# A two-layer graph kernel: the first pair of row blocks cut into two blocks of half the rows

## The chip, the cores and the metric

The kernel runs on one core of one Trainium2 chip. The metric is device time of one execution in microseconds, lower is better. The engines are TensorE (PE in the profile, its weight loads PEld), VectorE (DVE), ScalarE (ACT), GpSimd (POOL, which also issues most transfers) and SyncE (SP).

## The reference, cut to what matters

`N = M = 4096` rows and columns, `D = 64` features. `adj` is a 4096 x 4096 matrix of 0 and 1 with about 0.2% ones.

```python
h = relu(layernorm(x))
s = (h @ W) @ a1                      # one score per row
t = (entity_embs @ W) @ a2            # one score per column
e = leaky_relu(s[:, None] + t[None, :], 0.2)
e = where(adj > 0, e, -9e15)
att = softmax(e, axis=1)              # 4096 x 4096
x = x + elu(att @ entity_embs + h)
h = relu(layernorm(x))
x = x + (adj == 1) @ h + h
```

## The kernel before

Everything is held transposed: columns of `adj` lie on the 128 partitions in 32 column tiles, rows lie along the free axis. The 4096 rows are four **pairs** of two **halves** of 512 rows (`HALF`), and a **block** is one pair (`HALVES = (2, 2, 2, 2)`). A **step** n is one column tile of one block, 128 columns by 1024 rows; there are 4 x 32 = 128 steps. `adj` arrives as bf16 in 64 **chunks** of 512 KB, 16 to a block, two steps to a chunk, in a ring of 24 slots (`am`). POOL issues them, chunk q into the slot of chunk q - 24 once the steps of that one are made.

Per step:

- DVE makes `yp` (L819): max of the row's score `s8b` and the column's `t8neg`, plus the mask in `am`. Its output has four buffers (`YS`), so step n waits until TensorE is through with step n - 4 (`pv_done`).
- ACT takes the exponential in place (L593).
- PE adds the tile to the block's numerator `acc2` (L1077) and, at every odd step, two tiles to the denominators `dens` (L1092).

The exponent needs a shift for each row, an upper bound on its scores over its neighbours. For a block of rows it comes from this chain, which needs all chunks of that block: PE sums `gtab` against `am` (`biggest`, L926), DVE reads the sums (`read_sums`, L693, L694), PE transposes (`turn`, L938), DVE takes maxima (`largest`, L700) and computes the shift (`shifts`, L707 to L722), PE spreads it over the partitions (`v_rows`, L946), ACT copies it to `vx` (L520), and DVE puts it into the masks with an exclusive or, two chunks at a time (`put_shift`, L735). `lone_rows` (L744) treats a special case. For blocks 1 to 3 the chain runs inside the steps of the block before, at step numbers from `sum_at`, `read_at`, `TURN`, `LARGEST`, `SHIFTS`, `VROWS`. For block 0 it runs ahead of step 0.

Ahead of step 0 stand two more chains. The column scores and their **extremes** lead over DVE and two small PE instructions (L1021, L1024) to `gtab` (L663 to L674). The first layernorm goes pair by pair: **centring** on PE (L1016), squares on ACT, `variance` on PE (L878), the power -1/2 and a diagonal matrix on POOL (`spread_out`, L423 to L425), `deviation` on PE (L885), `normed` on DVE (L640) to `h0`. From `h0` PE makes the row scores (`s_rows`, L906; `s_cols`, L913). PE also sums the entities (L1033, called esum here).

After a block's steps, `FIN` says at which steps of the next block its sums are inverted, weighted, added to `x`, normalized again and split into three bf16 parts `h3` (`inverses`, `spread`, `weighted`, `rows_on`, `centred`, `variance_again`, `normed_again`, `rests`, `lasts`).

The second layer is 32 **pieces** (`ORDER`), each one column group of 512 times one pair, four parts of six matmuls (`neighbours`, L1005). Eighteen are placed inside the steps by `PIECE_AT`, part i at step `PIECE_AT[v] + i`, and fourteen run after the last step. Pieces in `DIRECT` read the mask in the ring itself, so they must be done before `put_shift` changes that chunk: L733 makes DVE wait for them. Others get a copy of the mask by a transfer of its own (`edges`).

All order on an engine is the order of the code; each engine runs its list in order and waits on semaphores.

## Time and profile before

| what | value |
|---|---|
| median of 3 runs | 409.32 us (408.3 to 410.26) |
| the profiled execution | 408.06 us, span 406.3 us |
| PE busy | 350.4 us (86%) |
| DVE busy | 304.3 us (75%) |
| ACT busy | 183.1 us (45%) |
| POOL busy | 112.2 us (28%) |
| step 0 begins on DVE | 63.18 us |
| step 32 begins on DVE | 131.88 us |
| last step's matmuls end on PE | 362.7 us |

The span runs from the first to the last instruction of the core. Busy shares are means over the whole span, so the table says nothing about which engine ends last in a given stretch; for that the time-ordered views are read.

### The profile page before, as it was taken

The page shows a single profiled execution, that of the slowest core. Times are in us where ns is not written, and L with a number is a line of the kernel's source. Part 1 is how long each engine was busy: PE and PEld are TensorE (multiplying, and loading weights), DVE is VectorE, ACT ScalarE, POOL GpSimd, SP SyncE. Part 2 cuts the span into 40 slices and gives each one's busy share as a digit, 9 for nine tenths or more (in the row PEclk, how much of TensorE's full clock was granted, in tenths as well). Part 3 has the DMA queues.
Part 4 walks back from the last instruction along what each step waited for, and adds up shares of the span by engine and source line. Part 5 has one row for each costly group of instructions (what it writes and reads, how often), then busy time and mean ns, then how long its engine had stood idle before and what let it go on. Part 6 is the DMA issues. An engine that isn't in the chain of part 4 may idle for free.

```text
span 406.3 us, 5556 instructions
## 1 busy us (share of the span) xinstructions
PE 350.4 (86%) x2291; PEld 124.7 (31%) x2295; DVE 304.3 (75%) x303; ACT 183.1 (45%) x206; POOL 112.2 (28%) x165
## 2 busy tenths in 40 slices
PE   0568535999887779999898999997989999999996
PEld 0244211323121113233232332332323333334564
DVE  3282069968999998988999879699997899833211
ACT  1130114645646566744476556535556456532100
POOL 4189901101102114134311131202013199000500
PEclk9977955999999999999999999999999999999999
DMA  7999999875858987775598967999999990000011
GB/s 221 238 213 212 214 213 213 138 128 106 154 105 116 169 129 123 123 137 92 97 146 133 149 104 120 99 100 96 108 89 107 107 98 2 2 2 0 2 53 52
DMA packets 15848, 47.85 MB, mean 118 GB/s; under 512 B 1552, under 2 KB 1616, under 8 KB 15568
## 3 DMA queue, kind: packets, MB, share of 16 engines
q0 software_dynamic: 14656, 44.05, 71.1%
q1 hardware_dynamic: 1168, 3.46, 2.3%
q8 instruction: 18, 0.29, 0.3%
q14 instruction: 6, 0.05, 0.0%
HBM read 111.46 MB, written 1.05 MB: 277 GB/s over the span
## 4 chain that ended last, share of the span: by engine, by line
PE 51%; DVE 27%; issue 6%; POOL 6%; another core or an unknown queue 3%; ACT 3%; DMA 3%; SPq 1%; DVEq 0%; ACTq 0%
PE pb L1077 17%; DVE yp L819 15%; PE pb L1005 9%; PE pb L1092 8%; PE pa L1005 8%; DVE am L735 7%; DMA xs<-xt 3%; ACT yp L593 2%; POOL yp L425 2%; POOL rstd L424 2%; PE pa L926 2%; PE pa L906 2%; PE pb L1016 1%; PE pa L970 1%
## 5 line engine op out<-in xcount | busy, mean ns | idle before, releaser
L593 ACT ACTIVATE yp<-yp,tbias 128x1024 f32<-128x1024 f32 x128 | 146.3, 1149 | 112.6 <-DVE yp L819 110.6
L819 DVE SCALAR_TENSOR_TENSOR yp<-s8b,t8neg,am 128x1024 f32<-128x1024 f32 x128 | 160.9, 1295 | 15.3 <-PE pb L1092 14.7
L1077 PE MATMUL pb<-yp,enta 128*64 128x512 f32 x512 | 136.1, 617 | 24.3 <-ACT yp L593 23.4
L387 POOL DMA_DIRECT2D am<-adj_t x64 | 35.2, 557 | 151.7 <-DVE yp L819 151.3
L735 DVE TENSOR_TENSOR am<-am,vx 128x4096 uint16<-128x4096 uint16 x32 | 73.6, 2299 | 2.2 <-ACT vx L520 1.4
L1092 PE MATMUL pb<-yp,onesf 128*32 128x512 f32 x512 | 68.3, 605 | 0.1
L1077 PEld LDWEIGHTS pb<-yp,enta 128*64 128x64 f32 x512 | 29.1, 136 | 93.8 <-ACT yp L593 68.2
L1005 PE MATMUL pb<-am,h 128*64 128x512 bf16 (+1 forms) x432 | 55.1, 379 | 0.0
L1005 PEld LDWEIGHTS pb<-am,h 128*64 128x64 bf16 x432 | 26.3, 110 | 39.5 <-issue 28.7
L396 POOL DMA_DIRECT2D am<-adj_t x16 | 11.5, 717 | 61.6 <-DVE yp L819 61.6
L1005 PE MATMUL pa<-am,h 128*64 128x512 fp8e4 x240 | 28.2, 380 | 0.0
L926 PE MATMUL pa<-am,gtab 128*32 128x512 bf16 x256 | 19.7, 388 | 3.6 <-DMA am<-adj_t 3.6
L471 POOL TENSOR_TENSOR am<-am,eyeb 128x128 fp8e4<-128x128 fp8e4 x24 | 22.5, 971 | 0.0
L1092 PEld LDWEIGHTS pb<-yp,onesf 128*32 128x32 f32 x512 | 10.1, 108 | 36.9 <-issue 35.9
L1005 PEld LDWEIGHTS pa<-am,h 128*64 128x64 bf16 x240 | 14.5, 110 | 16.0 <-issue 7.7
L693 DVE TENSOR_SCALAR gmax<-pa,wk 128x1024 f32<-128x1024 int32 (+1 forms) x5 | 5.3, 1068 | 12.3 <-PE pa L926 12.3
L1016 PE MATMUL pb<-xs,mats 128*128 128x512 f32 x8 | 5.7, 880 | 9.6 <-DMA xs<-xt 9.6
L926 PEld LDWEIGHTS pa<-am,gtab 128*32 128x32 bf16 x256 | 6.5, 97 | 21.2 <-issue 20.7
L460 POOL TENSOR_SCALAR rstd<-rstd 128x8 f32<-128x8 f32 x4 | 1.0, 246 | 40.0 <-ACT rstd L548 40.0
L776 DVE TENSOR_TENSOR rs<-pa,rstd 128x512 f32<-128x512 f32 x4 | 2.8, 692 | 11.1 <-POOL rstd L461 11.1
L520 ACT CAST vx<-pa 128x512 bf16<-128x512 f32 x8 | 4.3, 580 | 13.6 <-remote 13.6
L640 DVE TENSOR_TENSOR h<-h,pb 128x512 f32<-128x512 f32 x4 | 2.7, 686 | 9.4 <-PE pb L885 9.4
(145 smaller groups left out, 259.4 us busy)
## 6 DMA issues: line engine op xcount, KB each, us to landing
am<-adj_t POOLq DMA_DIRECT2D x80, 512.0 KB, 7.7
edge<-adj_t POOLq DMA_DIRECT2D x4, 512.0 KB, 10.3
enta<-ent SPq DMA_DIRECT2D x1, 1040.0 KB, 5.2
xs<-xt SPq DMA_DIRECT2D x1, 1024.0 KB, 11.1
out<-yp SPq DMA_DIRECT2D x4, 256.0 KB, 2.0
mats<-eye SPq DMA_DIRECT2D x1, 256.0 KB, 6.7
wt_sb<-w_t SPq DMA_DIRECT2D x1, 32.0 KB, 2.2
a_sb<-a_cols SPq DMA_DIRECT2D x1, 0.5 KB, 2.1
```

The lines of the kernel that those rows point to most:

```text
L387: pool.dma_start(am[:, q % RING], adj_t[q]).then_inc(landed[q % RING], 16)
L396: pool.dma_start(edges(v).rearrange("p (c t) i -> p c (t i)", c=2), adj_t[q:q + 2].rearrange("c p n -> p c n")).then_inc(edges_in[v], 16)
L424: link(g.tensor_tensor(rstd0[:, p], rstd0[:, p], mhalf[:], ALU.pow))
L471: g.tensor_tensor(e, e, eyeb[:], ALU.add, saturate=False).then_inc(own_ready, 1)
L593: sc.activation(y, y, ACT.Exp, bias=tbias[:, at:at + 1]).then_inc(exp_done, 1)
L735: v.tensor_tensor(at, at, vx[:, b % 2, 0:width(b)].bitcast(U16).unsqueeze(1).to_broadcast([P, 2 * tiles(b), width(b)]), ALU.bitwise_xor).t ...
L819: v.scalar_tensor_tensor(out=yp[:, n % YS, 0:W], in0=s8b[:, b % 2, 0:W], scalar=t8neg[:, at:at + 1], in1=am[:, (chunk0[b] + c) % RING, jt ...
L926: mm = t.matmul(pa[g * KC:(g + 1) * KC, i], gtab[:, tile_at(b, jt)], am[:, (chunk0[b] + jt // T) % RING, at:at + HALF], start=(k == 0), st ...
L1005: mm = t.matmul(gather(v)[s * D:(s + 1) * D, :], h3[:, jt, k * D:(k + 1) * D], masks(v, i, s), start=(v in OPENS and i == 0 and k == 0), s ...
L1016: t.matmul(pb[:, p], centre, xs[:, p], start=True, stop=True).then_inc(x0_ps, 1)
L1077: t.matmul(acc2(b)[s * D:(s + 1) * D, :], enta[:, tile_at(b, jt), 0:D], yp[:, n % YS, s * HALF:(s + 1) * HALF], start=(jt == 0), stop=(jt ...
L1092: mm = t.matmul(dens[at:at + 32, :], onesf[:, 0:32], yp[:, (n - 1 + r) % YS, s * HALF:(s + 1) * HALF], start=(jt == 1), stop=(jt == NT - 1 ...
```

## The change

The first pair of rows becomes two blocks of one half each: `HALVES = (1, 1, 2, 2, 2)`. A chunk of such a block holds four column tiles of 512 rows, and a step takes two of them, so that a step is again 128 x 1024 elements and there are again 128 steps: block 0 is steps 0 to 15, block 1 steps 16 to 31, and blocks 2 to 4 are what blocks 1 to 3 were. Line numbers here are those of before.

- DVE and ACT issue two instructions of 512 instead of one of 1024 at each of steps 0 to 31.
- Block 0's shifts need 8 chunks. Block 1's chain is in block 0's steps: `read_sums` after step 4, `turn` at 5, `largest` and `shifts` after 7, `v_rows` at 8. For what is now block 2: sums at steps 6 to 24, then 25, 26, 28, 29.
- On PE the extremes' two instructions stand ahead of the centring, the centring of a pair between the variances, and `s_rows`, `s_cols` ahead of the esum.
- The two blocks' numerators and denominators are put together by four matmuls (`combined`) at step 34, copied out by ACT at 35. The end work of the first pair is two steps later each time, and the first six pieces start two steps later (`PIECE_AT` 49, 53, 59, 63, 69, 73 for 47, 51, 57, 61, 67, 71).
- `s_rows` of the next pair is one call for both halves, at steps 18, 48 and 78. POOL issues chunks 18 to 23 after its twelve small esum instructions.
- `mats` grows from four to five 128 x 128 matrices.

```diff
-HALVES = (2, 2, 2, 2)
+HALVES = (1, 1, 2, 2, 2)
...
+    NC_STEPS = [NT * m // 2 for m in HALVES]
+    start_of = [sum(NC_STEPS[:b]) for b in range(NB + 1)]
...
     def landed_at(q):
-        n = max(0, int((q - 16) * 1.2)) if q < 32 else 0
+        n = max(0, int(q * 1.29 - 15.5)) if q < 32 else 0
...
-        n = landed_at(chunk0[b] + (k + 1) * HALVES[b] - 1) + 1
+        n = landed_at(chunk0[b] + (k + 1) * HALVES[b] - 1) + (b >= 3)
...
-    SROWS = [(8, 10), (13, 15), (13, 15)]
-    TURN = [max(read_at(b + 1) - b * NT + 1, SROWS[b][-1] + 3) for b in range(NB - 1)]
+    SROWS = [None, 2, 16, 14]
+    TURN = [read_at(b + 1) - start_of[b] + 1 for b in range(NB - 1)]
     LARGEST = [t + 2 for t in TURN]
-    SHIFTS = [t + 3 for t in TURN]
+    SHIFTS = LARGEST
...
+        both = mats[:, 4, 0:D]
+        four = mats[:, 4, D:D + 32]
...
             def sums_out(b):
-                act.wait_ge(pv_done, (b + 1) * NT)
...
+                act.wait_ge(pv_done, start_of[b + 1])
+                if single(b):
+                    if b == 0:
+                        act.wait_ge(esp_ready, 1)
+                    sc.copy((tm, rs)[b][:], dens).then_inc(den_sb, 2)
+                    sc.copy((ta, num)[b][:], acc2(b)).then_inc(num_sb, 2)
+                    return
...
+            def combined():
+                act.wait_ge(comb_ps, 1)
+                sc.copy(inv, turned[D:P]).then_inc(inv_in, 1)
+                sc.copy(num[:], pb[:, 3]).then_inc(comb_sb, 1)
...
-                y = yp[:, n % YS, 0:width(b)]
-                at = tile_at(b, jt)
-                sc.activation(y, y, ACT.Exp, bias=tbias[:, at:at + 1]).then_inc(exp_done, 1)
+                m = 2 // HALVES[b]
+                for r in range(m):
+                    y = yp[:, n % YS, r * HALF:r * HALF + width(b)]
+                    at = tile_at(b, jt * m + r)
+                    e = sc.activation(y, y, ACT.Exp, bias=tbias[:, at:at + 1])
+                e.then_inc(exp_done, 1)
...
-            for p in range(NP):
-                normed(p)
+            normed(0)
+            normed(1)
             dve.wait_ge(eyeb_ready, 1)
             read_sums(0)
+            normed(2)
             largest(0, 0)
-            largest(0, 1)
             shifts(0)
             put_shift(0, 0)
             lone_rows(0)
+            normed(3)
...
+            def combined():
+                pe.wait_ge(num_sb, 4)
+                pe.wait_ge(den_sb, 4)
...
+                for s in range(2):
+                    t.matmul(pb[s * D:(s + 1) * D, 3], both, (ta, num)[s][:], start=True, stop=True,
+                             tile_position=(0, s * D))
+                for s in range(2):
+                    at = D + 32 * s
+                    mm = t.matmul(turned[at:at + 32], four, (tm, rs)[s][:], start=True, stop=True, tile_position=(0, at))
+                mm.then_inc(comb_ps, 1)
```

What the code's order now is on two engines, at the places that the prediction speaks of. The columns are line, operation, output <- inputs, size.

TensorE ahead of step 0, in the kernel before (`yp,onesf 64x512` is `deviation`, `am,gtab` is `biggest`, `enta` is the esum, `mats,m` and `d,onesf` are the extremes):

```order
L1016 MATMUL pb<-xs,mats 128x512 x4
L878 MATMUL pa<-mats,yp 128x2 x4
L1021 MATMUL pa<-mats,m 2x128
L1024 MATMUL pa<-d,onesf 128x2
L878 MATMUL pa<-mats,yp 128x2 x12
L885 MATMUL pb<-yp,onesf 64x512 x4
L1033 MATMUL pa<-enta,onesf 128x260 x8
L926 MATMUL pa<-am,gtab 32x512 x8
```

And of the change, from the same place to the point where the esum stands:

```order
L1097 MATMUL pa<-mats,m 2x128
L1100 MATMUL pa<-d,onesf 128x2
L1091 MATMUL pb<-xs,mats 128x512 x2
L936 MATMUL pa<-mats,yp 128x2 x4
L1091 MATMUL pb<-xs,mats 128x512
L936 MATMUL pa<-mats,yp 128x2 x4
L1091 MATMUL pb<-xs,mats 128x512
L936 MATMUL pa<-mats,yp 128x2 x8
L943 MATMUL pb<-yp,onesf 64x512 x2
L984 MATMUL pa<-am,gtab 32x512 x8
L962 MATMUL pa<-h,w 128x512 x2
L969 MATMUL pa<-w8s,h 128x2 x4
```

The extremes no longer stand behind the four centring matmuls, one pair's `deviation` instead of two is ahead of the first sums, and the row scores are ahead of the esum, which follows one call of `biggest` later.

VectorE from the first sums to the first step, in the kernel before (the seven small instructions of `shifts` stand between the two pieces shown):

```order
L693 TENSOR_SCALAR gmax<-pa,wk 128x512
L694 SCALAR_TENSOR_TENSOR gmax<-pa,gmax 128x512
L693 TENSOR_SCALAR gmax<-pa,wk 128x512
L694 SCALAR_TENSOR_TENSOR gmax<-pa,gmax 128x512
L700 TENSOR_REDUCE um<-pa 128x4 x2
...
L722 TENSOR_TENSOR vd<-eyeb,vb 128x512 x2
L735 TENSOR_TENSOR am<-am,vx 128x4096
L744 TENSOR_SCALAR rows<-vx 3x1024
L819 SCALAR_TENSOR_TENSOR yp<-s8b,t8neg,am 128x1024 x2
```

And of the change:

```order
L744 TENSOR_SCALAR gmax<-pa,wk 128x512
L745 SCALAR_TENSOR_TENSOR gmax<-pa,gmax 128x512
L694 TENSOR_TENSOR h<-h,pb 128x512
L751 TENSOR_REDUCE um<-pa 128x4
...
L773 TENSOR_TENSOR vd<-eyeb,vb 128x512
L786 TENSOR_TENSOR am<-am,vx 128x4096
L795 TENSOR_SCALAR rows<-vx 3x512
L694 TENSOR_TENSOR h<-h,pb 128x512
L876 SCALAR_TENSOR_TENSOR yp<-s8b,t8neg,am 128x512 x4
```

One half's chain is left ahead of step 0, and `normed` of pairs 2 and 3 (`h<-h,pb`) stands between its parts.

TensorE where the first pieces of the second layer begin, in the kernel before, from step 47 (`am,h 64x512` is a part of a piece, `yp,enta` the numerator of a step):

```order
L1077 MATMUL pb<-yp,enta 64x512 x2
L1005 MATMUL pb<-am,h 64x512 x6
L1092 MATMUL pb<-yp,onesf 32x512 x4
L1077 MATMUL pb<-yp,enta 64x512 x2
L1005 MATMUL pb<-am,h 64x512 x6
```

And of the change, from step 46 (the first row holds steps 46 and 47):

```order
L1161 MATMUL pb<-yp,enta 64x512 x4
L1176 MATMUL pb<-yp,onesf 32x512 x4
L962 MATMUL pa<-h,w 128x512 x2
L1161 MATMUL pb<-yp,enta 64x512 x4
L1082 MATMUL pb<-am,h 64x512 x6
```

The first part of piece 0 moved from step 47 to step 49, so its last part is now in step 52 and that of piece 1 in step 56. The masks that these two read are changed by DVE's `put_shift` behind steps 53 and 57 in both kernels.

## Rows read from the trace of the kernel before

**Rows 1.** The page: span, and one engine line and one group.

```profile
span 406.3 us, 5556 instructions
...
PE 350.4 (86%) x2291; PEld 124.7 (31%) x2295; DVE 304.3 (75%) x303; ACT 183.1 (45%) x206; POOL 112.2 (28%) x165
...
L926 PE MATMUL pa<-am,gtab 128*32 128x512 bf16 x256 | 19.7, 388 | 3.6 <-DMA am<-adj_t 3.6
```

**Rows 2.** Windows (steps 0-31, 32-63): PE, PEld, DVE, ACT, POOL busy; clock, DMA, GB/s.

```profile
63.18:131.88 68.70, 60.42 (x367) 16.47 (x370) 62.89 (x56) 38.46 (x37) 9.32 (x17) 0.95 0.78 134
131.88:204.90 73.02, 64.97 (x407) 18.81 (x406) 67.68 (x64) 42.10 (x46) 20.19 (x26) 1.00 0.74 123
```

**Rows 3.** The chain that ended last: start us, us, what.

```profile
14.31 5.71 PE pb L1016 x8
...
39.35 1.91 POOL yp L425
41.30 1.08 PE pb L885 x4
42.93 1.06 PE pa L906 x4
44.53 1.00 PE pb L913 x8
45.73 13.60 another core or an unknown queue
```

**Rows 4.** Timeline up to the first step (start us, us, engine, line).

```profile
12.19 0.15 DVE L650 TENSOR_SCALAR m<-m 128x1 f32<-128x1 f32 x1
...
23.28 1.79 DVE L664 TENSOR_SCALAR kq<-kq 128x32 f32<-128x32 f32 x1
...
27.55 1.22 DVE L674 TENSOR_TENSOR gtab<-gtab,pw 128x1024 bf16<-128x1024 bf16 x1
...
32.98 5.00 PE L1033 MATMUL pa<-enta,onesf 128*128 128x260 f32 x16
...
50.53 1.04 PE L926 MATMUL pa<-am,gtab 128*32 128x512 bf16 x8 [3.60 <-DMA am<-adj_t]
...
56.49 0.17 DVE L707 TENSOR_SCALAR vq<-um 128x8 f32<-128x8 f32 x1
...
59.34 1.19 ACT L520 CAST vx<-pa 128x512 bf16<-128x512 f32 x2 [13.62 <-remote]
60.64 2.29 DVE L735 TENSOR_TENSOR am<-am,vx 128x4096 uint16<-128x4096 uint16 x1 [1.39 <-ACT vx L520]
...
63.18 2.46 DVE L819 SCALAR_TENSOR_TENSOR yp<-s8b,t8neg,am 128x1024 f32<-128x1024 f32 x2
```

**Rows 5.** Three windows of 3 us, columns as in group 2.

```profile
24.00:27.00 3.00, 2.25 (x15) 2.16 (x14) 2.79 (x8) 1.27 (x4) 2.84 (x5) 0.71 1.08 216
...
33.00:36.00 3.00, 3.00 (x10) 2.46 (x9) 0.69 (x1) 0.00 (x0) 2.92 (x2) 0.58 1.08 214
...
69.00:72.00 3.00, 3.00 (x24) 0.90 (x24) 2.56 (x4) 2.30 (x3) 0.53 (x1) 0.90 0.99 178
```

**Rows 6.** DVE groups by shape: one over the whole run, one of steps 0-31.

```profile
L694 DVE SCALAR_TENSOR_TENSOR gmax<-pa,gmax 128x512 f32<-128x512 int32 x2 | 1.4, 692 | 0.1
...
L819 DVE SCALAR_TENSOR_TENSOR yp<-s8b,t8neg,am 128x1024 f32<-128x1024 f32 x33 | 40.8, 1279 | 5.6 <-PE pb L1092 5.3
```

**Rows 7.** Timeline of DVE, then of PE, around steps 53 and 57.

```profile
179.62 2.29 DVE L735 TENSOR_TENSOR am<-am,vx 128x4096 uint16<-128x4096 uint16 x1
...
186.31 1.28 DVE L693 TENSOR_SCALAR gmax<-pa,wk 128x1024 f32<-128x1024 int32 x1 [1.70 <-PE pa L926]
...
191.16 2.29 DVE L735 TENSOR_TENSOR am<-am,vx 128x4096 uint16<-128x4096 uint16 x1
...
178.36 0.82 PE L1005 MATMUL pb<-am,h 128*64 128x512 bf16 x6
...
182.52 0.82 PE L1005 MATMUL pb<-am,h 128*64 128x512 bf16 x6
```

420 lines of the change are left out of this document (230 added, 190 removed).

## The prediction

> **What bounds the kernel now.** I read the page first. TensorE is busy for 350.4 of 406.3 us [rows 1], so time can only come out of its first quarter or out of its work. The windows by steps come next: in steps 0 to 31 VectorE is busy 62.89 of 68.70 us and TensorE 60.42; in steps 32 to 63 it is 67.68 and 64.97 of 73.02 [rows 2]. Both are nearly full, VectorE a little more. Since step n needs step n - 4's buffer back, neither runs away from the other, and an earlier step 0 moves everything behind it, the tail too, as long as no new wait stands in the way. Third, the chain that ended last shows what sets step 0: centring until 20.0, POOL's diagonals until 41.26, then `deviation`, the row scores and the column scores on TensorE (1.08, 1.06, 1.00 us), and then 13.6 us that the view gives to an unknown queue [rows 3]. The timeline says what that is: TensorE waits 3.60 us for the last chunk of the block, which ends at 50.53, and its last sums end at 51.57; from there sums, transposes, maxima, shifts, the copy to `vx` and the first `put_shift` lead to step 0 at 63.18 [rows 4]. So the last chunk of 16 ends the wait, and behind it come 11.6 us that nothing covers.
>
> **Part 1: when step 0 starts.** Only 8 chunks are needed. The transfers run at 216 GB/s [rows 5], 2.4 us for 512 KB; chunk 15 landed at 50.5, so chunk 7 lands near 31. That is ahead of what follows, so the transfers no longer decide, and three chains must be followed.
>
> *Extremes.* Their values are ready at 12.34 [rows 4], but their matmuls stood behind the centring that ended at 20.0 [rows 3] and the first variance, and `gtab` was done at 28.77 [rows 4]. Turned at once, they gain 8.2 us: 20.5, or 19 if L664's 1.79 us (its neighbours of the same size take 0.2; it ran beside POOL's diagonal) goes too. Not last any more.
>
> *Centring.* Variance 0 now waits for two of four centrings, between half of 5.71 and, at the lower clock of their start, 3.4 us; it comes 2.3 to 2.9 us earlier and so do POOL's four diagonals: the fourth is ready near 39. The fifth matrix of `mats` is 64 KB, 0.3 us. TensorE has the four variances behind it near 25.3, `deviation` 0 at 26.4, and VectorE's multiplication (0.69, as L694 of that size [rows 6]) gives `h0` at 27.1.
>
> *TensorE's list from there.* `s_rows` 1.06 and `s_cols` 1.00 [rows 3]; 3 calls of four sums, at 19.7/256 us a matmul [rows 1] 0.3 each, the first two while `h0` is made: 29.5. Then the esum. It took 5.00 us from 32.98 [rows 4], half of it at the lower clock: the mean granted was 0.71 in 24 to 27 and 0.58 in 33 to 36 [rows 5], which puts the rise at 35.5. That is 2.5 us at 1.2 GHz and 2.5 at 2.4, so 3.75 if all at 2.4 and 7.5 if all at 1.2. I take 3.75, because in the new order TensorE has no hole longer than 1 us between 14.3 and here, where before its clock fell after holes: 33.2. `deviation` 1 is 1.1, five calls of sums 1.5: 35.8.
>
> *Behind the last sums.* Before: 51.57 to 63.18, 11.6 us. Up to the shifts at 56.49 it was 4.9 us for two halves in turn; for one it is two reads of 0.7, four transposes of 1.1 together and a maximum of 0.7 = 3.6, so 1.3 less. ACT's 1.19 us for two copies [rows 4] becomes 0.6. Added: `normed` 3 with 0.7, and 0.4 for small VectorE instructions beside POOL's last diagonal. `deviation` 2 and `normed` 2 lie beside the reads and the transposes: cost 0.7 without that cover. 11.6 - 1.3 - 0.6 + 0.7 + 0.4 = 10.8, so step 0 at 46.6: **16.6 us earlier**. Bounds: 45 (quick turns at 2.4 GHz) to 52 (esum at 1.2 GHz and 2 us for the rest of TensorE's list).
>
> **Part 2: steps 0 to 31.** Block 1's own chain, once ahead of step 0, is now in VectorE's steps: reads 1.4, maximum 0.7, small ones and one `vd` 2.1, lone rows 0.3: **+4.5 us** on the fuller engine. TensorE gets half a block's sums (2.5), transposes and shift row (1.0) too; it had 8.3 us free [rows 2] and loses the slack, no more. Two instructions of 512 for one of 1024: L694 takes 0.692 at 512 and L819 1.279 at 1024 [rows 6]. By durations that is 0.10 for each of 32 steps, 3.4 us; by starts (63.18 to 65.58 for two steps, 1.20 each [rows 4], against 0.61 for a 512) 0.6. These run unlinked, so I take the starts more: **+1.0**. ACT has 30 us free [rows 2]; 32 more instructions cost nothing. VectorE's waits, 5.8 us (68.70 - 62.89), 5.6 of them in front of L819 [rows 6], were made where TensorE had sums, row and column scores in steps 5 to 12 together; these are spread now, but block 0's sums and transposes come while TensorE is still at 1.2 GHz, and `read_sums` stands right behind step 4: 4.5 left, **-1.3**, bounds -4 and +3.
>
> The Trainium skill, page "VectorE: DVE Perf Modes", section on the TRN2 errata, speaks against this split: an instruction that reads SBUF pays a fixed cost each time, by its table 58 cycles at 0.96 GHz on VectorE. By it the split would be 1.9 us instead of my 1.0, an estimate from that page; the rows lie on both sides of it.
>
> **Part 3: steps 32 to 47.** `combined` is two matmuls like a step's numerator and two like its denominators, 2.0 us on TensorE; one VectorE instruction of 0.7 goes. It stands at step 34, where TensorE in steps 32 to 63 has 8 us free [rows 2], and behind it in the queue waits step 34's numerator, whose buffer VectorE needs at step 38. ACT's two copies replace three. **+0.3**, 2.0 without the cover. The end work's two steps of delay reach only `h3`, and the pieces move with it.
>
> **Part 4: a new wait at steps 53 and 57.** Before, piece 0 ended at 179.2 and `put_shift` behind step 53, which needs it, began at 179.62: 0.4 us of margin though three steps lie between, because TensorE trails. Now piece 0 ends in step 52. The part of a piece in that step ended at 183.3 [rows 7]; with two parts fewer ahead of it (0.75 each) it would be at 181.8. VectorE gets there at 178.2 to 179.6 and waits 2.2 to 3.6 us. What is behind it in its queue is step 54, for which TensorE runs dry; the 1.70 us that VectorE later waited for the sums [rows 7] is saved, so some 0.5 us is lost. At step 57 nothing is saved: piece 1 ends in step 56, and VectorE, which began that `put_shift` at 191.16 without a wait, waits about 2.1. Together **+2.6**, bounds 0 (TensorE trails less) and 5. Later pieces keep their margins.
>
> **Sum.** -16.6 + 4.5 + 1.0 - 1.3 + 0.3 + 2.6 = -9.5. The profiled execution took 408.06, so 398.6; it lies 0.3% below the median of 409.32, and for the median of the new kernel I give 399.
>
> **Rivals.**
>
> *The clock falls as before (0.2).* In 24 to 27 the mean was 0.71 [rows 5]. If it falls at 25 again, the esum costs 3.75 more and what stands around it up to 2: step 0 near 52, 404. For: each variance still waits for ACT. Against: the list between is full.
>
> The Trainium skill, page "TensorE: Matmul & The Clock Gate", section "What's actually happening", says that the low clock is the default and activity releases it. By that rule the fuller list holds 2.4 GHz and the forecast stands; the fall at 25 after a sparse stretch agrees.
>
> *The waits shrink more (0.2).* Without part 4's wait and with 2.5 us less in part 2: 394. For: pieces start later, so TensorE trails less.
>
> *The transfers decide after all (0.08).* By 2.4 us each, chunk 12 lands at 43 and is needed near 45, chunk 17 at 55.5 for step 6 near 60, chunk 23 at 70 for step 14 near 77. One that comes 3 us after its need gives 402. Against: POOL issues 18 to 23 while 16 and 17 are still on their way.
>
> *Slower: TensorE stays at 1.2 GHz in the first two blocks (0.05).* Step 0 comes when TensorE has been nearly idle for 8 us, and the small blocks hold VectorE longer per step. At 1.2 GHz two steps cost it some 6.6 us (3.7 and 2.0, and a share of sums) against 4.4 for VectorE: 1.1 a step. After 9 steps the gain is gone, with all 32 it is 433. Against: 1.00 was not far after step 0, the mean of 69 to 72 was 0.90 [rows 5], six to nine us behind the start of step 0.
>
> The forecast has 0.47. Its own range is 395 to 402; the range that leaves out 2 in 10 takes in the fall of the clock and most of the shrinking: 392.5 to 404.5. Measurement tells 0.5%, 2 us, from no change. Faster 0.94, within 0.03, slower 0.03: the last two are the long stay at 1.2 GHz and a stack of the bounds.
>
> **What would show it.** Right: first L876 near 46.6, esum of 3.6 to 4 us, no TensorE wait for a chunk of more than 1 us, step 32 near 119.5 and a wait of 2 to 4 us on PE in front of `put_shift` behind steps 53 and 57. Wrong: a first step after 50, a step 32 more than 73 us behind step 0, or TensorE idle behind step 100 for more than before.

## The result and the profile after

The changed kernel takes 407.83 us (median of 20, 404.77 to 414.96) against 408.29 (median of 20, 407.26 to 410.3) for the kernel before. The ratio is 0.9948, with a 95% interval of 0.9925 to 0.9971: 2.1 us faster, where 399 us had been forecast. Six of the 20 executions, 412.5 to 415.0 us, are left out of the ratio as slow ones; over all twenty the medians differ by 0.5 us and the means not at all (408.6 us both).

The profiled execution took 405.43 us, the one of before 408.06. The page of the changed kernel, its head and some lines of the 40 slices:

```profile
span 403.6 us, 5645 instructions
PE 353.0 (87%) x2303; PEld 122.1 (30%) x2303; DVE 307.0 (76%) x342; ACT 190.3 (47%) x241; POOL 119.1 (29%) x165
PE   1697597889879897987898999997989999999996
DVE  3804899899989998787699888898998999823211
PEclk9989799999989989998699999999999999999999
```

Against [rows 1] TensorE is busy for 2.6 us more, VectorE for 2.7, ScalarE for 7.2 and GpSimd for 6.9. What is new is in the line PEclk: behind the first quarter, where before nothing but 9s stood, there are falls in the slices near 120, 140 and 190 us, and in the last of them PE shows 7 and 8 and DVE 7 and 6.

The windows by steps, up to step 0, steps 0 to 31, 32 to 63, and 64 to 95. Columns: window, its length, then busy us and instructions of PE, PEld, DVE, ACT and POOL, the mean granted clock, the DMA share and GB/s.

```profile
0.00:45.88 45.88, 28.42 (x148) 14.22 (x148) 20.92 (x47) 8.71 (x21) 31.81 (x54) 0.93 0.98 222
45.88:121.58 75.70, 63.27 (x383) 16.39 (x385) 71.28 (x100) 45.49 (x72) 22.05 (x29) 0.95 0.94 176
121.58:204.65 83.07, 72.07 (x430) 19.82 (x428) 69.30 (x65) 44.40 (x48) 18.09 (x27) 0.92 0.66 109
204.65:281.90 77.25, 72.47 (x494) 23.82 (x494) 68.76 (x66) 43.93 (x48) 13.95 (x20) 1.00 0.91 115
```

Step 0 starts at 45.88 instead of 63.18: 17.3 us are won. Steps 0 to 31 then take 75.7 us instead of 68.7, and steps 32 to 63 take 83.1 instead of 75.4 (the window in [rows 2] ends at 204.90, where the `put_shift` ahead of step 64 starts; step 64 itself began at 207.26). That is 7.0 and 7.7 us given back. By the starts of step 48, 168.6 before and 158.5 now, nearly all of the second loss lies in steps 48 to 63: steps 32 to 47 take 36.9 us for 36.8, and steps 48 to 63 take 46.2 for 38.6. From step 64 to the end both kernels take the same time within 0.1 us. So the sum is -17.3 + 7.0 + 7.7 = -2.6, the difference of the profiled executions.

The timeline to step 0 (start, duration, engine, line, operation; count; idle time before it and what ended it):

```profile
14.77 3.68 PE L1091 MATMUL pb<-xs,mats 128*128 128x512 f32 x4 [0.70 <-DMA xs<-xt]
18.06 1.23 DVE L728 TENSOR_TENSOR gtab<-gtab,pw 128x1024 bf16<-128x1024 bf16 x1
19.09 1.10 PE L1091 MATMUL pb<-xs,mats 128*128 128x512 f32 x2
30.11 3.77 PE L1121 MATMUL pa<-enta,onesf 128*128 128x260 f32 x16
34.81 1.26 PE L984 MATMUL pa<-am,gtab 128*32 128x512 bf16 x20
42.75 2.32 DVE L786 TENSOR_TENSOR am<-am,vx 128x4096 uint16<-128x4096 uint16 x1 [1.17 <-ACT vx L559]
45.88 2.72 DVE L876 SCALAR_TENSOR_TENSOR yp<-s8b,t8neg,am 128x512 f32<-128x512 f32 x4
45.99 7.62 POOL L478 TENSOR_TENSOR esum<-esp,mats 128x65 f32<-128x65 bf16 x1
```

The table is ready at 19.3 instead of 28.8, the sum over the entities takes 3.77 us instead of 5.00, and no sum waits for a chunk: the wait of 3.60 us in [rows 4] has no successor. TensorE's clock did fall here too, from 25.0 to 28.5 us, but it was up again before the esum. The same view at steps 53 to 63, VectorE's waits and TensorE's holes:

```profile
172.78 2.29 DVE L786 TENSOR_TENSOR am<-am,vx 128x4096 uint16<-128x4096 uint16 x1 [3.73 <-PE pb L1082]
184.52 2.29 DVE L786 TENSOR_TENSOR am<-am,vx 128x4096 uint16<-128x4096 uint16 x1 [2.21 <-PE pb L1082]
189.24 1.98 PE L1161 MATMUL pb<-yp,enta 128*64 128x512 f32 x4 [2.55 <-ACT yp L644]
194.43 1.98 PE L1161 MATMUL pb<-yp,enta 128*64 128x512 f32 x4 [1.76 <-ACT yp L644]
199.55 2.48 DVE L876 SCALAR_TENSOR_TENSOR yp<-s8b,t8neg,am 128x1024 f32<-128x1024 f32 x2 [3.81 <-PE pb L1176]
```

VectorE waits 3.73 and 2.21 us for pieces 0 and 1, as predicted. But there is a third line of that kind: at 199.55 it waits 3.81 us for a buffer, for TensorE. Windows of 5 us show what stands ahead of it:

```profile
180.00:185.00 5.00, 5.00 (x38) 2.00 (x34) 2.79 (x3) 2.30 (x2) 0.57 (x1) 1.00 0.64 108
185.00:190.00 5.00, 2.45 (x20) 0.69 (x20) 4.90 (x8) 1.62 (x2) 0.00 (x0) 0.89 0.42 83
190.00:195.00 5.00, 3.00 (x8) 0.50 (x6) 4.86 (x9) 1.72 (x2) 1.49 (x3) 0.50 0.03 3
195.00:200.00 5.00, 5.00 (x22) 1.07 (x20) 1.19 (x2) 2.58 (x4) 2.27 (x4) 0.59 0.91 161
```

While VectorE stood at `put_shift`, it issued no step; TensorE ran dry behind it (2.45 of 5 us busy from 185 on), and then its granted clock went to 0.50, the level of 1.2 GHz. Four of its step matmuls took 1.98 us instead of 1.08 and it was late in its turn, and VectorE waited once more. By this trace one wait brings another; how far that holds is what the experiments ask.

### The profile page after: what moved, and what is told of

Read it like the earlier page. It is cut to its first block, busy times and chain, and to the rows that moved or that the text cites. A ratio compares the mean times of both kernels' runs of the same rounds, so it can differ in the third digit from the quotient of the medians.

```text
span 403.6 us, 5645 instructions
## 1 busy us (share of the span) xinstructions
PE 353.0 (87%) x2303; PEld 122.1 (30%) x2303; DVE 307.0 (76%) x342; ACT 190.3 (47%) x241; POOL 119.1 (29%) x165
## 4 chain that ended last, share of the span: by engine, by line
PE 54%; DVE 27%; issue 7%; ACT 6%; DMA 3%; POOL 1%; SPq 1%; DVEq 0%; ACTq 0%
PE pb L1161 17%; DVE yp L876 14%; PE pb L1082 9%; PE pb L1176 9%; PE pa L1082 8%; DVE am L786 6%; ACT yp L644 4%; DMA xs<-xt 3%; PE pa L984 2%; PE pb L1091 1%; DVE um L751 1%; PE pa L1047 1%; PE pa L1053 1%; PE pa L962 1%; PE pa L1121 1%
## 5 line engine op out<-in xcount | busy, mean ns | idle before, releaser
L644 ACT ACTIVATE yp<-yp,tbias 128x1024 f32<-128x1024 f32 (+1 forms) x160 | 152.1, 975 | 123.0 <-DVE yp L876 121.5
L876 DVE SCALAR_TENSOR_TENSOR yp<-s8b,t8neg,am 128x1024 f32<-128x1024 f32 (+1 forms) x160 | 164.7, 1075 | 15.8 <-PE pb L1176 15.3
L1161 PE MATMUL pb<-yp,enta 128*64 128x512 f32 x512 | 138.8, 627 | 28.8 <-ACT yp L644 28.4
L1176 PE MATMUL pb<-yp,onesf 128*32 128x512 f32 x512 | 70.7, 625 | 0.0
L1161 PEld LDWEIGHTS pb<-yp,enta 128*64 128x64 f32 x512 | 29.2, 137 | 97.4 <-ACT yp L644 68.7
L1176 PEld LDWEIGHTS pb<-yp,onesf 128*32 128x32 f32 x512 | 10.2, 109 | 38.5 <-issue 36.9
L984 PE MATMUL pa<-am,gtab 128*32 128x512 bf16 x256 | 21.5, 416 | 0.0
L499 POOL TENSOR_SCALAR rstd<-rstd 128x8 f32<-128x8 f32 x4 | 1.5, 387 | 38.1 <-ACT rstd L599 38.1
L500 POOL TENSOR_TENSOR rstd<-rstd,mhalf 128x8 f32<-128x8 f32 x4 | 10.4, 2604 | 0.3
L919 DVE SCALAR_TENSOR_TENSOR yp<-pa,xs 128x512 f32<-128x512 f32 x2 | 1.4, 692 | 10.0 <-PE pa L1082 10.0
L478 POOL TENSOR_TENSOR esum<-esp,mats 128x65 f32<-128x65 bf16 x2 | 8.3, 4127 | 0.2
```

What stands on the lines that cost most here:

```text
L478: return g.tensor_tensor(dst, esp[:, 0], eyef[:, k:k + 1].to_broadcast([P, D + 1]), ALU.mult)
L500: g.tensor_tensor(rstd[:], rstd[:], mhalf[:], ALU.pow).then_inc(rstd_ready, 1)
L644: e = sc.activation(y, y, ACT.Exp, bias=tbias[:, at:at + 1])
L876: y = v.scalar_tensor_tensor(out=yp[:, n % YS, r * HALF:r * HALF + W], in0=s8b[:, pair(b) % 2, cols(b)], scalar=t8neg[:, at:at + 1], in1=a ...
L984: mm = t.matmul(pa[g * KC:(g + 1) * KC, first[b] % 2 + i], gtab[:, tile_at(b, jt)], am[:, (chunk0[b] + jt // T) % RING, at:at + HALF], sta ...
L1161: t.matmul(acc2(b)[s * D:(s + 1) * D, :], enta[:, at, 0:D], yp[:, n % YS, s * HALF:(s + 1) * HALF], start=(jt == 0), stop=final, tile_posi ...
```

## The experiments

Theory A: what is missing lies in part 4, the pieces that end one step before their `put_shift`, with the fall of TensorE's clock that follows. Rivals: the price of the split (C), block 1's own chain (D), the pair's combination. In the diffs, a kernel is called by what it starts from.

**b_pieces_late: part 4 alone, in the kernel before.** It has the six changed places of the pieces and nothing else.

```diff
-PIECE_AT = (47, 51, 57, 61, 67, 71, 79, ...
+PIECE_AT = (49, 53, 59, 63, 69, 73, 79, ...
```

> The kernel before with nothing changed but the first six pieces two steps later (49, 53, 59, 63, 69, 73). Theory A, the late pieces: VectorE's put_shift behind steps 53 and 57 now waits for pieces that end in steps 52 and 56, TensorE then runs dry and its clock falls; this alone costs what the changed kernel gave back in steps 32 to 63, so 411 to 415 us against 408.3, with two waits of 2 to 4 us on PE in front of L735. Theory B, the rest of the change (the earlier start, the joining of the two blocks, the fuller VectorE) makes TensorE idle and the clock fall: then this kernel stays at 408 to 409.5, with waits in front of L735 but no fall of the clock.

414.25 us against 408.07, ratio 1.0166 (1.014 to 1.0193). The two rows of its timeline:

```profile
181.74 2.29 DVE L735 TENSOR_TENSOR am<-am,vx 128x4096 uint16<-128x4096 uint16 x1 [3.74 <-PE pb L1005]
193.48 2.29 DVE L735 TENSOR_TENSOR am<-am,vx 128x4096 uint16<-128x4096 uint16 x1 [2.22 <-PE pb L1005]
```

They are the waits of the changed kernel to 0.01 us, and there were none in [rows 7]. The move of the pieces costs 6 us by itself, in a kernel that has none of the rest. That is A's total, but its profile (5.1 us longer) shows only a part of A's way. Steps 48 to 63 grow by 3.8 us here, against 7.5 in the changed kernel. The clock falls once behind the second wait, for 3.4 us from 198.3, where the changed kernel has it low for 10.2 us from 188.9, and VectorE's third wait, of 3.81 us, is missing. Another 1.7 us arise in steps 64 to 95, which the changed kernel doesn't lose; no run shows why. So A holds for the two waits; that they alone bring the third is not shown.

**a_pieces_48 and a_put_later: the wait taken away in the changed kernel, in two ways.** The first lets pieces 0 and 1 start one step earlier. The second leaves them and puts off block 2's two xors that need them.

```diff
-PIECE_AT = (49, 53, 59, ...
+PIECE_AT = (48, 52, 59, ...
```

```diff
-                if jt % SUB == 1 and c + 2 < HALVES[b] * NQ:
+                later = {21: None, 25: None, 22: 12, 27: 14} if b == 2 else {}
+                if jt in later:
+                    if later[jt] is not None:
+                        put_shift(b, later[jt])
+                elif jt % SUB == 1 and c + 2 < HALVES[b] * NQ:
```

> The changed kernel with pieces 0 and 1 at steps 48 and 52 in place of 49 and 53, so that each ends two steps ahead of the put_shift that needs it and not one. Theory A: most of the two waits (3.7 and 2.2 us) goes and the clock does not fall near 189 us: 399 to 402 us against 405.3. Theory B: the waits go, but the clock falls all the same and VectorE waits elsewhere: 404 to 405.5.

> The changed kernel with the two put_shift calls that wait for pieces moved on VectorE, from behind steps 53 and 57 to behind steps 54 and 59; the pieces stay where they are. Theory A: the waits shrink to under 1 us and the time is 399 to 403 us, though put_shift, reads and shifts now stand closer together, which can starve TensorE once for 2 us. Theory B: 404 to 406.

405.77 us, ratio 0.9896 (0.9856 to 0.9936), and 405.3 us, ratio 0.9884 (0.9843 to 0.9926). The waits at `put_shift` are down to 1.09 and 0.35 us, but only 2.1 and 2.5 us of the 6 came back; A had expected 399 to 403. Both intervals still overlap that of the changed kernel, the second one barely. In a_pieces_48 B's signs came. TensorE waited 1.73 us at 190.85 for the `vd` of the next block's shifts, the clock fell at 192.5 all the same, and VectorE waited at step 62:

```profile
197.40 2.48 DVE L876 SCALAR_TENSOR_TENSOR yp<-s8b,t8neg,am 128x1024 f32<-128x1024 f32 x2 [2.87 <-PE pb L1176]
```

In a_put_later the clock holds there and that wait is gone. Steps 32 to 63 take 78.4 us, and two waits for TensorE stand behind a stretch at 1.2 GHz from 158.0 to 164.8:

```profile
168.36 2.48 DVE L876 SCALAR_TENSOR_TENSOR yp<-s8b,t8neg,am 128x1024 f32<-128x1024 f32 x2 [3.17 <-PE pb L1180]
172.95 1.28 DVE L876 SCALAR_TENSOR_TENSOR yp<-s8b,t8neg,am 128x1024 f32<-128x1024 f32 x1 [2.11 <-PE pb L1180]
```

**b_split: the two instructions of 512 alone, in the kernel before**, for steps 0 to 31 on VectorE and ScalarE.

```diff
-                v.scalar_tensor_tensor(out=yp[:, n % YS, 0:W], in0=s8b[:, b % 2, 0:W], ...
+                w = HALF if b == 0 else W
+                for r in range(W // w):
+                    e = jt % T * W + r * w
+                    y = v.scalar_tensor_tensor(out=yp[:, n % YS, r * w:(r + 1) * w], ...
```

> The kernel before with each instruction of 1024 on VectorE and ACT in steps 0 to 31 issued as two of 512, nothing else. In the changed kernel two such instructions start every 1.33 us against 1.20 for one. Theory C: this price is the split's own, 0.13 us a step on the fuller engine, so steps 0 to 31 take 4 us longer and the time is 411.5 to 413. Rival D: the steps got longer by block 1's chain and its waits; the split itself costs 1 us or less and the time is 408.5 to 409.5.

412.93 us, ratio 1.0114 (1.0093 to 1.0136). Its windows for steps 0 to 31 and 32 to 63:

```profile
63.03:134.23 71.20, 60.61 (x369) 16.09 (x370) 66.85 (x88) 44.35 (x69) 9.28 (x17) 0.96 0.77 132
134.23:209.52 75.29, 67.30 (x429) 19.50 (x428) 69.87 (x65) 43.66 (x47) 21.39 (x28) 1.00 0.74 124
```

Against [rows 2] VectorE is busy for 3.96 us more, 0.124 us for each of 32 steps, and its waits shrink by 1.5, so the stretch grows by 2.5 us. This is near the bound that the durations gave (0.10), not the one that I took from the starts. C is right for a part. The whole kernel lost 4.6 us by the ratio and 3.4 in the profiled execution. Steps 32 to 127 take what they took before; 1.2 us of the 3.4 lie behind the start of the last step (51.7 us for 50.6), and no run shows why.

**a_combined_twice: the pair's combination made twice.**

```diff
-                for s in range(2):
+                for s in (0, 1, 0, 1):
```

> The changed kernel with the four matmuls that put the pair's parts together made twice (the second pass writes the same values over the first): some 2 us more of TensorE work at step 34. The prediction costed one pass at +0.3 us, 2.0 without cover. If cover holds, the time stays within 1 us of 407.8 and step 48 within 0.5 us of 158.5. If the 2 us come through, step 48 is near 160.5 and the time near 410; then one pass is worth about 2 us and a part of what steps 32 to 63 took too long.

407.89 us, ratio 1.0002 (0.9968 to 1.0035); step 48 at 159.4 and step 64 at 205.7 us, where the two profiles of the changed kernel have 158.5 and 158.0, 204.6 and 206.1. Counted from step 32, step 48 comes 1.1 and 1.7 us later than in those two, so a part of the 2 us came through there; at the end it isn't told from none (this kernel's interval and the changed one's just overlap). What lets this rival fall is the changed kernel itself: steps 32 to 47, with the combination in them, take 36.9 us for 36.8 before.

**b_extremes_first and a_order_back: the order of the front, alone in the kernel before, and taken back in the changed one.**

```diff
+            pe.wait_ge(m2_ready, 1)
+            t.transpose(turned[0:2, 2 * P:3 * P], m2[:, 0:2], eyef).then_inc(m2t_ps, 1)
...
             pe.wait_ge(ld_x, 16)
             for p in range(NP):
                 t.matmul(pb[:, p], centre, xs[:, p], start=True, stop=True).then_inc(x0_ps, 1)
             variance(0)
-            pe.wait_ge(m2_ready, 1)
-            t.transpose(turned[0:2, 2 * P:3 * P], m2[:, 0:2], eyef).then_inc(m2t_ps, 1)
```

> The kernel before with one part of the change alone: TensorE turns the extremes ahead of the centring. The blocks stay. By the prediction the last chunk of the first block (landed at 50.5 us) sets step 0, so the table of ready values should come some 8 us earlier (near 20 us instead of 28.8) and step 0 stay within 0.5 us of 63.2: time within 0.5% of the kernel before. Rival: the earlier sums shift POOL's and TensorE's work so that step 0 moves by 2 us or more, and the halved first block is not what the 17.3 us come from alone.

> The changed kernel with TensorE's order of before in the front: four centrings and a variance, then the extremes, then the other variances. The table of ready values comes near 28 us instead of 19.3; the row scores and the sums of block 0 wait for it. By the prediction's chains the list behind the table (row and column scores, sums, colsum, 8 us) then starts at 28 instead of 26: step 0 at 47.5 to 50, 2 to 4 us later, and the time 2 to 4 us over the changed kernel's beside it. Rival: the esum and the diagonals of POOL hide it, step 0 within 0.7 us of 45.9, and the order of the extremes is worth nothing here either.

In the kernel before the new order gives nothing: 410.25 us, ratio 1.0024 (1.0003 to 1.0046). Its timeline has the table at 19.2, and then the same wait for the same chunk:

```profile
17.99 1.22 DVE L674 TENSOR_TENSOR gtab<-gtab,pw 128x1024 bf16<-128x1024 bf16 x1
50.74 1.04 PE L926 MATMUL pa<-am,gtab 128*32 128x512 bf16 x8 [3.98 <-DMA am<-adj_t]
63.39 1.27 DVE L819 SCALAR_TENSOR_TENSOR yp<-s8b,t8neg,am 128x1024 f32<-128x1024 f32 x1
```

In the changed kernel, taking the order back costs more than the 2 to 4 us expected: 413.28 us beside 409.51 for the changed kernel in the same set, 5.0 us by the two ratios (1.009, 1.0053 to 1.0127, against 0.9968), and in the profiled execution, the longest of the eight, step 0 8.3 us later:

```profile
19.51 0.95 PE L936 MATMUL pa<-mats,yp 128*128 128x2 f32 x8
27.19 1.23 DVE L728 TENSOR_TENSOR gtab<-gtab,pw 128x1024 bf16<-128x1024 bf16 x1
35.70 6.59 PE L1119 MATMUL pa<-enta,onesf 128*128 128x260 f32 x16
54.19 2.72 DVE L876 SCALAR_TENSOR_TENSOR yp<-s8b,t8neg,am 128x512 f32<-128x512 f32 x4
```

Block 0's first sums start at 28.84 instead of 26.08. The table, ready at 28.4, explains 2.3 us of that at most: the sums begin right behind `deviation`, without a wait. The other 5.5 us arise behind them, where TensorE had gone to 1.2 GHz at 24.4 us and stayed there until 41.4 (the sum over the entities takes 6.59 instead of 3.77 us). So the order is worth something only with the halved block; the halving brings step 0 from 63.18 to 54.19 without it. By this one execution the larger part of what the order brings goes with the clock; no run has the one without the other. b_extremes_first showed the price of a fall too, by chance. Its 12 executions are 407.85 to 408.42 at a mean granted clock of 0.962 (five) and 410.22 to 410.71 at 0.954 (seven). The profiled one is of the second kind, and its clock falls at 153 us, where that of [rows 2] had held 1.00. Its steps 32 to 47 take 38.1 us for 36.8, with a new wait of VectorE for a buffer of 1.30 us at 157.98. So this stretch, 3.4 us at 1.2 GHz, costs some 1.4 us. The 2.1 us between the two groups hold more than this one stretch: a mean clock 0.008 lower is some 6.5 us at 1.2 GHz, and the lower group has no profile.

**a_fill and a_later_fill: TensorE kept busy in its holes.** Matmuls with all-zero weights are added to a sum that is open, so nothing but TensorE's time changes. The first is the changed kernel (4 to 6 such matmuls ahead of steps 29, 46, 54, 58, 59), the second a_put_later (ahead of 29, 46, 59, 60).

```diff
+                if n in FILL:
+                    pe.wait_ge(zeros_in, 1)
+                    for _ in range(FILL[n]):
+                        t.matmul(acc2(b)[0:D, :], zeros[:], gtab[:, 0:HALF // KC].rearrange("p t k -> p (t k)"),
+                                 start=False, stop=False, tile_position=(0, 0))
                 pe.wait_ge(exp_done, n + 1)
```

> The changed kernel with 23 extra TensorE matmuls (512 columns, bf16, all-zero weights, added to a sum that is open) in the holes in which TensorE idled 1.5 to 2.6 us before it waits for the exponential: 5 ahead of step 29, 4 ahead of 46, 4 ahead of 54, 6 ahead of 58, 4 ahead of 59. The result is unchanged. Theory E (the falls of TensorE's clock behind these holes are themselves what costs a part of steps 32 to 63): the stretches at 1.2 GHz near 117, 141 and 189 us are gone, steps 32 to 63 take 78 to 80 us instead of 83.1, the time is 3 to 5 us under the changed kernel's 407.8, and its runs spread less. Rival F (the falls only accompany holes that the wait makes; VectorE is what is late): the granted clock stays up but step 64 comes within 1 us of 204.6, time 407 to 409; and if TensorE reaches these places late, the extra work costs up to 5 us.

> The changed kernel with both xors of block 2 one and two steps later (as in the run before, 405.3 us) and 18 such zero matmuls: 5 ahead of step 29, 6 ahead of 46, 5 ahead of 59, 3 ahead of 60, where TensorE still idled 2.0 to 2.5 us and its clock fell at 117.0 and 158.0 us. Theory E: no stretch at 1.2 GHz between 110 and 200 us, the waits of 3.2 and 2.1 us in front of VectorE's steps at 168 and 173 us vanish, time 401 to 403. Rival F: no gain over 405.3, or a loss of up to 4 us from the added TensorE work.

a_fill: 405.63 us, ratio 0.9928 (0.9897 to 0.9958); of the three falls that were to go only the one near 117 did (140.6 and 191.8 are still there). Step 64 comes 2.1 us earlier, and a new fall at 274 takes 1.6 of that back in the profiled execution. Its interval overlaps that of the changed kernel: not decided. a_later_fill: **399.95 us, ratio 0.9784 (0.9752 to 0.9816)**. By the ratios that is 4.1 us under a_put_later, whose interval it doesn't touch; the two profiled executions are only 1.5 us apart (400.70 and 402.15), and a part of the 4.1 may be the groups of executions told of further down. Its windows for the same two stretches:

```profile
45.28:121.30 76.02, 64.08 (x394) 17.01 (x400) 71.30 (x99) 45.49 (x72) 22.06 (x29) 0.95 0.95 178
121.30:198.20 76.90, 69.95 (x435) 20.15 (x430) 69.67 (x65) 44.40 (x48) 21.47 (x27) 0.98 0.69 115
```

Steps 32 to 63 are at 76.9 us, 6.2 less than in the changed kernel and 1.5 less than in a_put_later, with more matmuls on TensorE. Behind step 48 there is no fall before 270, VectorE's wait of 3.17 us is down to 0.43, and steps 48 to 63 take 39.3 us for 42.1; the one of 2.11 stays, and a fall at 124.1 comes anew. The falls of the clock are not a mere sign of the holes. The expected 401 to 403 was too careful.

What one fall costs is read best where nothing else differs. Four kernels have the same instructions in steps 32 to 47: a_best, this one, a_best2 and a_best3. They take 36.3, 37.6, 37.6 and 38.5 us, with none, one, one and two stretches of 3.4 us at 1.2 GHz. And the two profiles of the changed kernel (a_again is the second) take 79.7 and 81.4 us for steps 64 to 95, without and with such a stretch. That is 1.3 to 1.7 us for one. The third wait, the one of 3.81 us, goes with the time that the clock is low between steps 58 and 62. In the profiles of the halved block it is 2.1 to 2.9 us with 3.4 us low (a_fill, a_pieces_48), 2.9 to 3.7 with 6.8 (five of them, a_again with 2.89), 3.8 and 3.9 with 10.2 (the changed kernel, a_fill_front), and it is missing where the clock held (a_put_later, a_later_fill, the three a_best). Only b_pieces_late has 3.4 us low and no such wait.

**a_again and a_fill_front: the changed kernel once more, and with its last two holes ahead of step 0 filled** (10 zero matmuls ahead of the shift row, 8 ahead of step 0).

> The changed kernel once more, as the neighbour of the runs of this call: 405 to 409 us for most executions, some at 411 to 415. Its executions fall into groups 6 us apart whose mean granted clock is no lower in the slow group, so the falls of the clock do not make these groups; they only make steps of 1 to 2 us within one.

> The changed kernel with zero matmuls in the two holes of TensorE ahead of step 0: 10 ahead of the shift row of block 0 (idle 3.24 us) and 8 ahead of step 0 (idle 2.90). Theory E: the stretches at 1.2 GHz at 42.1 and 48.9 us (3.4 us each) are gone, step 0 stays within 0.5 us of 45.9, step 8 comes 1 to 2 us earlier than 65.7 and the time is 1 to 3 us under the changed kernel's beside it. Theory S (the groups 6 us apart come from where the clock is low in the front): no execution above 409. Rival: VectorE, busy 71.3 of 75.7 us from step 0 on, sets these steps; step 32 stays within 0.7 us of 121.6 and the groups remain.

409.51 us (404.89 to 413.08), ratio 0.9968 (0.993 to 1.0007); and 410.42 us (404.83 to 415.22), ratio 0.9944 (0.9899 to 0.9988). The fall at 42 is gone, the one at 49 stayed, step 0 is still at 45.9 and step 8 at 65.7, where 1 to 2 us had been expected. All profiles with the halved block take 75.5 to 76.1 us for steps 0 to 31, whatever the clock did in them: where VectorE sets the pace, TensorE's clock costs half a microsecond at most. The executions far above the others stayed.

**a_best: both fillings, the later xors and six zero matmuls ahead of step 91.**

> All that helped together: xors of block 2 later, zero matmuls ahead of steps 29, 46, 59 and 60 (399.95 us in the run before), and besides 10 ahead of the shift row, 8 ahead of step 0 and 6 ahead of step 91, where TensorE still idled 2.0 us and the clock fell at 270.8. Theory E: no stretch at 1.2 GHz at 42, 124 or 271 us except at most one, time 396 to 399. Rival: VectorE sets the pace in these stretches, 399.5 to 401.

Three executions at 398.0 to 398.4 us and three at 403.0 to 404.2 (median 400.65, ratio 0.9766, 0.9709 to 0.9823), so half of them where 396 to 399 had been expected, and the profiled one is of the upper three:

```profile
14.50 3.78 PE L1099 MATMUL pb<-xs,mats 128*128 128x512 f32 x4 [0.45 <-DMA xs<-xt]
19.64 2.06 PE L1099 MATMUL pb<-xs,mats 128*128 128x512 f32 x2
23.05 2.05 PE L1099 MATMUL pb<-xs,mats 128*128 128x512 f32 x2
50.91 2.72 DVE L880 SCALAR_TENSOR_TENSOR yp<-s8b,t8neg,am 128x512 f32<-128x512 f32 x4
```

Here is what sets such an execution apart. The centrings behind the first take 2.06 us for two matmuls where the changed kernel above has 1.10, the level of 1.2 GHz against 2.4, and step 0 starts at 50.91, 5 us later. The clock had not risen during the centring. (The granted clock can't be read here: the view shows 1.00 ahead of its first record, at 34 us in this execution and at 18 in the changed kernel's.)

**a_warm and b_warm: TensorE kept busy ahead of the centring**, with 22 zero matmuls, in the changed kernel and in the one before.

```diff
+            keep_busy(5)
             pe.wait_ge(arep_ready, 1)
...
+            keep_busy(17)
```

> The changed kernel with 22 all-zero matmuls (512 columns, bf16) on TensorE ahead of the centring: 5 at the start and 17 behind the first two matmuls, where it idled 7.85 us. Theory M (the group 5 to 6 us higher is made by a clock that first rises at 34 instead of 18 us): the rise comes before 14 us in every execution, the four centrings and variances run at 2.4 GHz, step 0 comes at 43 to 45.3 instead of 45.9, and no execution is above 409; median 404 to 406. Rival N (the groups have another cause, POOL beside VectorE or the transfers): a third of the executions still lies 5 to 6 us above the others.

> The kernel before with the same 22 zero matmuls in the front. By the prediction its step 0 waits for chunk 15, which lands at 50.5 us, and then for work at 1.2 GHz: an earlier rise of the clock near 14 us changes nothing before the chunk, so step 0 stays within 1 us of 63.2 and the time within 0.5% of 408. Rival: its front is as sensitive to the clock as that of the changed kernel, and it gains 2 us or more.

a_warm: 408.52 us (404.69 to 414.35), ratio 0.9976 (0.9947 to 1.0005); a miss. The clock rose at 8.0 us, but TensorE still idled 2.48 us behind the zero matmuls, and it fell again at 14.8, in the centring. b_warm: 408.91 us, ratio 1.0016 (0.9994 to 1.0038), step 0 at 64.0, with a wait of 4.30 us for the last chunk. The time is as expected, but its clock was down again from 15.3 to 18.7 and from 22.1 to 35.8, so what a clock that stays up would do for this front is not shown; the wait for the chunk leaves it nothing to gain ahead of 51.

**a_best2: the same front with the later xors and the fillings of steps 29, 46, 59, 60 and 91.**

> The same 22 zero matmuls in the front, the xors of block 2 later and zero matmuls ahead of steps 29, 46, 59, 60 and 91: everything that helped, without the fillings right ahead of step 0 that gave nothing. Theory M: one group only, 396 to 398.5 us, no execution above 401. Rival N: two groups, 398 and 403.

401.83 us (398.84 to 403.28), ratio 0.9821 (0.9783 to 0.9859); a miss, for none was to be above 401 and three are. The profiled execution, 403.28, had the clock down from 15.4 to 32.4 us, behind a hole of 2.36, and step 0 at 49.57.

**a_warm2 and a_best3: the front with more of its holes filled**, 26 instead of 17 zero matmuls, 2 behind the transposition, 2 behind the limits and 3 ahead of the last variance; a_best3 has the later steps of a_best2 too.

> As the run before with zero matmuls in the front of the changed kernel, now without a hole in them: 26 instead of 17 behind the first two matmuls, 2 each behind the transposition and the limits, 3 ahead of the last variance. Theory M: the clock rises near 8 us and is not at 1.2 GHz between 12 and 24, centring and variances take 1.1 and 1.0 us each from the first on, step 0 at 43.5 to 45.5 in every execution, and none is more than 4 us above the lowest. Rival N: the spread of 404.7 to 414.4 us stays.

> The same front with the xors of block 2 later and zero matmuls ahead of steps 29, 46, 59, 60 and 91. Theory M: one group, 396.5 to 399 us. Rival N: two groups again, near 398 and 403.

a_warm2: six executions at 405.16 to 407.69 us and one at 411.56 (median 406.67, ratio 0.9931, 0.9906 to 0.9957). The profiled one is the one, in windows of 4 us:

```profile
10.00:14.00 4.00, 2.14 (x11) 0.81 (x9) 3.53 (x7) 0.15 (x1) 2.89 (x6) 0.99 1.05 297
14.00:18.00 4.00, 4.00 (x9) 1.72 (x8) 2.81 (x16) 0.00 (x0) 0.00 (x0) 0.50 1.06 213
22.00:26.00 4.00, 4.00 (x12) 2.72 (x11) 0.00 (x0) 1.56 (x4) 3.92 (x3) 0.50 1.06 213
34.00:38.00 4.00, 4.00 (x26) 2.78 (x23) 0.00 (x0) 1.16 (x3) 3.84 (x5) 0.95 1.06 213
```

Now with a granted clock to read: 0.50 from 14 to 34 us, and step 0 at 52.26. a_best3: **399.56 us (397.83 to 400.23), ratio 0.9765 (0.9738 to 0.9792)**, the six executions within 2.4 us of each other, three of them in the expected 396.5 to 399 and three at 400.1 to 400.2. Its front in the same windows:

```profile
10.00:14.00 4.00, 3.38 (x16) 1.42 (x14) 3.02 (x9) 0.00 (x0) 2.34 (x5) 1.00 1.06 280
14.00:18.00 4.00, 3.62 (x16) 1.87 (x14) 3.58 (x14) 1.53 (x4) 0.18 (x1) 1.00 1.06 213
22.00:26.00 4.00, 3.75 (x26) 1.67 (x26) 0.69 (x1) 0.60 (x3) 3.77 (x6) 1.00 1.06 213
34.00:38.00 4.00, 0.76 (x6) 0.42 (x4) 3.81 (x5) 0.00 (x0) 3.77 (x4) 1.00 1.06 213
```

Step 0 at 44.47, the earliest of all. The two fronts are the same code, and in their profiles they part at one hole, the wait for VectorE's `m` behind the 26 zero matmuls, first in a_warm2 and then in a_best3:

```profile
13.46 0.27 PE L1109 MATMUL pa<-mats,m 128*2 128x128 f32 x1 [1.86 <-DVE m L707]
12.46 0.27 PE L1117 MATMUL pa<-mats,m 128*2 128x128 f32 x1 [0.55 <-DVE m L711]
```

Behind 1.86 us the clock fell, behind 0.55 it held; why `m` came 1.0 us later is open. In the three profiles with the clock low through the centring (a_best, a_best2, a_warm2) step 0 is at 49.6 to 52.3, in a_order_back, low from 24.4 to 41.4, at 54.2, and in the ten others of the halved block at 44.5 to 46.0. In the changed kernel itself no such execution was profiled: that its group at 412.5 to 415.0 us is the same is read from the distance alone. Behind this filling one execution in 13 was a high one, against 10 of 32 of the changed kernel; too few ran to tell that from chance.

## Why the prediction was wrong

The profiled executions differ by -2.6 us where the sum had -9.5. Part by part, measured for forecast: step 0 -17.3 for -16.6; steps 0 to 31 +7.0 for +4.2; steps 32 to 47 +0.1 for +0.3; steps 48 to 63 +7.5 for +2.6; nothing behind them. So 4.9 us of the error are part 4's and 2.8 part 2's. (By the prediction's own 0.3% its 398.6 would be 399.8 for the median, not 399.)

- **Part 1, step 0 at 46.6: right.** It came at 45.88 in the profiled execution, with the esum at 3.77 us for 3.75, no wait for a chunk, and chunks 0 to 7 in time. The reason given for the esum was in part luck: TensorE had indeed no hole longer than 1 us from 14.8 to 33.8 us, but the clock fell all the same at 25.0, as the rival with 0.2 had it, and was up again at 28.5, before the esum. b_extremes_first and a_order_back show that the new order brings step 0 nothing without the halving, and about as much as the halving with it. The rival's step 0 "near 52" is seen too, in another way, with the clock low through the centring: 49.6 to 52.3 in three profiles of such fronts. By the times about a third of the changed kernel's executions may be of this kind.
- **Part 2, the split at +1.0: mis-sized.** b_split shows 0.124 us a step, 3.96 us, by durations as I had it at 3.4 and not by starts. In the timeline above, four instructions of 512 start 0.66 us apart (2.72 us for all four, 0.73 for one); my 0.61 stands in no row and is about half of the 1.20 of a 1024. The Trainium skill, page "VectorE: DVE Perf Modes", section on the TRN2 errata, would have said 1.9 us by the fixed cost in its table: nearer, still half. The same section says that this row of the table gives too little for one instruction, with about 150 cycles measured; by that it would be 5.0 us, an estimate from that page. The 3.96 lie between the two. The rest of part 2 was right: VectorE's work grew by 8.4 us, 4.0 of it the split and so 4.4 left for block 1's chain (4.5 predicted; no run has it alone), and its waits shrank by 1.4 (1.3 predicted). The prediction's own sign of being wrong, step 32 more than 73 us behind step 0, came with 75.7.
- **Part 3, +0.3: right.** Steps 32 to 47 grew by 0.1 us. Doubling the combination put 1.1 to 1.7 us on them, so a second one is not covered.
- **Part 4, +2.6: the step that failed.** The waits were seen right, 3.73 and 2.21 us against "2.2 to 3.6" and "about 2.1". The saving was seen right too: the 1.70 us in front of the sums are gone. What failed is what comes after: I took the second wait as the end of the matter. Each of the two leaves TensorE without work, for 1.90 and 2.55 us; behind the second its clock falls to 1.2 GHz for 10.2 us, and VectorE waits again, 3.81 us. Without this third wait steps 48 to 63 would be at 42.4 us, where b_pieces_late has 42.5. The bound of 5 us had no room for it: I had asked about the clock only up to step 0 and in the first two blocks, and behind step 32 left it at the 1.00 of [rows 2]. The move of the pieces alone costs 6.2 us (b_pieces_late), without the third wait. Other holes were followed by falls too: 2.30 us ahead of step 29 near 117 us and, in a_again, 2.48 ahead of step 46 near 158. But 1.90 us near 177 were not, and the fall at 141 had only 0.89 and 0.80 ahead of it, so the length of a hole alone doesn't tell.

With the wait removed and the holes filled (a_later_fill) steps 32 to 63 take 76.9 us, and the kernel 399.95. That this is close to 399 doesn't prove the rest of the sum: its steps 0 to 31 still cost 3.2 us more than forecast, and 1.7 us are lost behind step 64, with a fall at 271. Open are why the clock stays low three times as long in the changed kernel as in b_pieces_late, what part of the third wait comes from `put_shift` and what from the wait for `vd` (a_pieces_48), and the 1.2 us of b_split behind the last step.

## What to carry over

An own wait that is small by its row must be followed through the other engine: who runs dry behind it, whether that engine's clock holds, and who then waits for the slower engine. When two engines are nearly equally full, as here, a piece of work that ends one step before it is needed is too late; ask for the slack in steps by which TensorE trails. A front whose speed hangs on the clock has several levels from one execution to the next, so judge it by more than one profile, and don't read a difference of two medians as the price of one cause before stretches with the same instructions have been compared. Price a split instruction by its duration, not by half the interval of the long one.
